# Diagonal row maxima of causal attention: the mask added on VectorE instead of TensorE

## The chip, the cores and the metric

The kernel runs on one core of one Trainium2 chip. The metric is the time of one execution on the device, in microseconds (us), and the median of several. The engines are TensorE (PE in the profile; PEld is its weight loads), VectorE (DVE), ScalarE (ACT), GpSimd (POOL) and SyncE (SP), which issues most DMAs. PSUM is the memory that TensorE writes, in banks of 128 partitions by 512 numbers of 32 bits.

## The reference, cut to what matters

One decoder layer on 2048 tokens of width 256: an embedding whose table is made ternary, an attention block with three branches, and a mixture of eight experts of which two are taken. Only the attention's causal branches bear on the change. There are 16 heads, queries and keys of width 96, values of width 32:

```python
def _attn(q, k, v, causal):
    scale = 1.0 / math.sqrt(q.shape[-1])
    s = jnp.einsum('bhqd,bhkd->bhqk', q, k) * scale
    if causal:
        Tq, Tk = (s.shape[-2], s.shape[-1])
        mask = jnp.tril(jnp.ones((Tq, Tk), dtype=bool))
        s = jnp.where(mask, s, jnp.finfo(s.dtype).min)
    return jnp.einsum('bhqk,bhkd->bhqd', jax.nn.softmax(s, axis=-1), v)
...
a1 = _attn(q, k1, v1, causal=True)
a2 = _attn(q, ks, vs, causal=False)
a3 = _attn(q, kw, vw, causal=True)
out = g[:, 0] * a1 + g[:, 1] * a2 + g[:, 2] * a3
```

`a1` is the branch that the kernel calls LATENT, `a3` is WINDOW, and both cover all 2048 keys with the causal mask. `a2` is SELECT, on 64 chosen keys, without a mask.

## The kernel before

The program runs stage after stage: `embed`, `project`, `select`, `attend` (the 16 heads), `mix`, `experts`. The change lies in `attend`, plus one constant that `embed` makes.

**Two passes over the scores.** A softmax needs each query row's maximum before the exponentials. So `attend` computes the scores twice. The first pass takes maxima only: a max task ("max", h, b, q, c) has queries as PSUM's partitions. It multiplies query block q (128 queries) with up to 512 keys of key block c into one bank of `ps_x` (L1518), and VectorE reduces the bank to one number per query, `max_part[:, q, c]` (L1607). After a branch's last task VectorE folds the parts (L1611), TensorE turns the result (a "neg" task), and it goes by DMA into extra rows of the query operand. The second pass, `pe_scores` (L1485 to L1489), computes the scores again with keys as partitions, three products each since every operand is split into an upper and a lower half. ScalarE takes the exponential twice (L1471, L1473), GpSimd or VectorE subtracts the two for the lower half (L1392), and `pe_values` multiplies both with the values four units later (L1575, L1577).

**The mask.** Where a task's keys reach the diagonal (c == q // 4), the last 128 columns of its w columns are a triangle. TensorE adds the constant `mask_qk` (0 or -1e30) to them by one more product, of `mask_qk` with an identity of bf16 (L1521). w is 128, 256, 384 or 512 in turn. Per head and branch 16 of 40 max tasks are diagonal. The second pass has its own mask product (L1559), with `mask_kq`. The first maxima of head 0 in WINDOW are made in `select`, so `attend` has 31 x 16 = 496 diagonal max tasks.

**Order.** Each engine runs a list written out by hand. A head is 84 units: 44 of WINDOW and SELECT, then 40 of LATENT. In each unit TensorE issues the unit's scores, then the side tasks that `schedule` places there, then the values of four units before. Side tasks are this head's LATENT maxima (units 7 to 37, first half of the head), the next head's SELECT and WINDOW maxima (second half), the "neg" turns, and in heads 0 to 11 the projections for a later group of heads ("prep"). All side tasks share a ring of three banks, `ps_x`: a task waits until VectorE has read the task three before it (semaphore `x_read`). VectorE takes its side tasks in the same order, and between them its share of L1392, the outputs' first addition (L1668), and six steps that finish the head before (L1676 to L1691).

Names in the rows below: `head_first` holds `q_hi`, `q_lo`, `kw_hi` and `kw_lo` of even heads.

Of the kernel before, what the change touches and what calls it, by code (L numbers as in the profile page):

```python
# [12 lines left out]
BF16 = mybir.dt.bfloat16  # L13
I32 = mybir.dt.int32
ALU = mybir.AluOpType
ACT = mybir.ActivationFunctionType
AX = mybir.AxisListType

P = 128
# [12 lines left out]
MASKED = -1.0e30  # L32
CH = 512
# [56 lines left out]
def embed(nc, g, a, x, weight):  # L90
# [7 lines left out]
    with ExitStack() as ctx:  # L98
# [56 lines left out]
        def _(pool):  # L155
# [11 lines left out]
            cst.add(nc.gpsimd.memset(g.mask_kq[:], 0.0))  # L167
            cst.add(nc.gpsimd.memset(g.strict[:], 1.0))
# [6 lines left out]
                                            base=0, pattern=[[1, P]], channel_multiplier=-1))  # L175
            cst.add(nc.gpsimd.affine_select(out=g.strict[:], in_=g.strict[:], compare_op=ALU.is_gt, fill=0.0,
# [892 lines left out]
def attend(nc, g, a):  # L1069
# [7 lines left out]
    with ExitStack() as ctx:  # L1077
# [418 lines left out]
        def pe_task(pe, t):  # L1496

            n = XN[t]
            bank = ps_x[n % NX]
            if n >= NX:  # L1500
                pe.wait_ge(s["x_read"], n - NX + 1)
            if t[0] == "max":
# [8 lines left out]
                if b == SELECT:  # L1511
                    for r in range(8):
                        last = nc.tensor.matmul(bank[:, r * KEEP:(r + 1) * KEEP], q_hi[par][0:DQK, (8 * q + r) * P:(8 * q + r + 1) * P],
                                                ks_hi[par][0:DQK, 0:KEEP], start=True, stop=True)
                else:
                    w = min(CH, (q + 1) * P - c * CH)
                    diag = c == q // 4
                    last = nc.tensor.matmul(bank[:, 0:w], q_hi[par][0:DQK, q * P:(q + 1) * P], k_hi[b][par][0:DQK, c * CH:c * CH + w],  # L1518
                                            start=True, stop=not diag)
                    if diag:  # L1520
                        last = nc.tensor.matmul(bank[:, w - P:w], g.ident16[:], g.mask_qk[:], start=False, stop=True)  # L1521
# [74 lines left out]
        def dve_task(dve, t):  # L1596
            n = XN[t]
            bank = ps_x[n % NX]
            if t[0] == "max":
                _, h, b, q, c = t  # L1600
                dve.wait_ge(s["x"], n + 1)
                if b == SELECT:
                    ins = nc.vector.tensor_reduce(nm[:, NT + 8 * q:NT + 8 * q + 8],
                                                  bank[:].rearrange("p (q k) -> p q k", k=KEEP), axis=AX.X, op=ALU.max, negate=True)
                else:
                    w = min(CH, (q + 1) * P - c * CH)
                    ins = nc.vector.tensor_reduce(mpart[:, q, c:c + 1], bank[:, 0:w], axis=AX.X, op=ALU.max)  # L1607
# [693 lines left out]
def layer(nc, a, out):  # L2301
# [12 lines left out]
    with ExitStack() as ctx:  # L2314
# [3 lines left out]
        g.gates, g.onehot, g.inv = tile("gates", [P, 3]), tile("onehot", [QA, NB]), tile("inv", [P, 1])  # L2318
        with ExitStack() as mid:
# [85 lines left out]
```

## Time and profile before

| | |
|---|---|
| median of 3 runs | 2747.41 us (2745.13 to 2747.56) |
| the profiled execution | 2745.16 us |
| its span in the profile | 2743.4 us |
| TensorE busy | 2327.9 us (85%) |
| VectorE busy | 1815.3 us (66%) |
| ScalarE busy | 1743.7 us (64%) |
| GpSimd busy | 1622.2 us (59%) |

How to read it: a matmul's duration covers its way through the array, so two that follow each other overlap; what one costs the stream is seen from the starts. A row's bracket tells how long the engine had been idle and what ended it. "issue" means that nothing in the profile was waited for. `attend` runs from about 400 to 2340 us; ahead of it come the table scan and the projections, behind it `mix` and `experts`.

### The profile page before, as it was taken

How to read it: one execution, taken by the hardware profiler on the slowest of the kernel's cores; microseconds unless marked ns; L12 is line 12 of the kernel's file. 1: busy time of each engine (PE TensorE's matmuls, PEld its weight loads, DVE VectorE, ACT ScalarE, POOL GpSimd, SP SyncE). 2: the span in 40 equal slices, each digit the busy share in tenths (PEclk: the TensorE clock that was granted, in tenths of full speed). 3: DMA queues.
4: the chain of work that ended last, by engine and by line, in shares of the span. 5: the costliest groups of instructions: out<-in, count | busy, mean ns of one | idle time of the engine just before them, and what ended most of it. 6: DMA issues, size and time to landing. Idle time of an engine off the chain costs nothing. (4 is left out here: it accounts for less than half of the span.)

```text
span 2743.4 us, 38402 instructions
## 1 busy us (share of the span) xinstructions
PE 2327.9 (85%) x12402; PEld 1845.8 (67%) x12402; DVE 1815.3 (66%) x2824; ACT 1743.7 (64%) x3574; POOL 1622.2 (59%) x1430
## 2 busy tenths in 40 slices
PE   0178579999999999999999999999999997538885
PEld 0155346777777777777777777777777775538885
DVE  2557457686776868687776868677686773455553
ACT  3433226777777777777777777777778776116663
POOL 4055316667676666767676666766656665006885
PEclk9985569999999999999999999999999998759998
DMA  9757654325151533414251533232132110615776
GB/s 382 311 187 246 189 127 108 91 68 136 24 154 29 136 66 108 112 48 124 52 142 38 138 69 91 61 67 60 34 67 49 32 25 17 194 62 177 197 203 169
DMA packets 199860, 314.87 MB, mean 115 GB/s; under 512 B 95915, under 2 KB 130219, under 8 KB 186731
## 3 DMA queue, kind: packets, MB, share of 16 engines
q1 hardware_dynamic: 189947, 298.23, 37.9%
q0 software_dynamic: 9712, 14.18, 2.8%
q8 instruction: 99, 1.62, 0.3%
q14 instruction: 102, 0.84, 0.1%
HBM read 210.20 MB, written 101.75 MB: 114 GB/s over the span
## 5 line engine op out<-in xcount | busy, mean ns | idle before, releaser
L1392 POOL TENSOR_TENSOR p_lo<-prob,p_hi 128x512 fp32r<-128x512 f32 (+2 forms) x960 | 1092.3, 1145 | 630.0 <-ACT p_hi L1473 544.7
L1471 ACT ACTIVATE prob<-ps_s 128x512 f32<-128x512 f32 (+4 forms) x1344 | 722.8, 538 | 465.8 <-PE ps_s L1489 303.0
L1607 DVE TENSOR_REDUCE max_part<-ps_x 128x1 f32<-128x128 f32 (+1 forms) x1240 | 713.4, 606 | 195.9 <-PE ps_x L1518 128.0
L1473 ACT ACTIVATE p_hi<-ps_s 128x512 fp32r<-128x512 f32 (+3 forms) x1344 | 718.5, 535 | 1.6
L1392 DVE TENSOR_TENSOR p_lo<-prob,p_hi 128x512 fp32r<-128x512 f32 (+1 forms) x320 | 308.0, 962 | 129.8 <-ACT p_hi L1473 124.4
L1575 PE MATMUL ps_o<-p_hi,v_win 128*128 128x512 f32 (+3 forms) x640 | 251.9, 394 | 8.5 <-DVE p_lo L1392 8.5
L1575 PE MATMUL ps_o<-p_hi,v_lat 128*128 128x512 f32 (+3 forms) x640 | 242.6, 379 | 0.0
L1577 PE MATMUL ps_o<-p_lo,v_win 128*128 128x512 f32 (+3 forms) x640 | 234.6, 367 | 0.0
L1577 PE MATMUL ps_o<-p_lo,v_lat 128*128 128x512 f32 (+3 forms) x640 | 234.1, 366 | 0.0
L1668 DVE TENSOR_TENSOR raw_o<-ps_o,low_sum 32x512 f32<-32x512 f32 x192 | 131.4, 684 | 78.9 <-ACT low_sum L1456 74.5
L1518 PE MATMUL ps_x<-k_hi,head_first 96*128 96x512 f32 (+2 forms) x320 | 120.6, 382 | 29.0 <-DVE max_part L1607 28.0
L1518 PE MATMUL ps_x<-k_hi,q_hi 96*128 96x512 f32 (+2 forms) x320 | 120.8, 383 | 26.7 <-DVE max_part L1607 26.0
L1575 PEld LDWEIGHTS ps_o<-p_hi,v_win 128*128 128x128 f32 x640 | 124.1, 194 | 27.3 <-DVE p_lo L1392 13.7
L1577 PEld LDWEIGHTS ps_o<-p_lo,v_lat 128*128 128x128 f32 x640 | 121.8, 190 | 19.6
L1575 PEld LDWEIGHTS ps_o<-p_hi,v_lat 128*128 128x128 f32 x640 | 122.2, 191 | 18.2 <-POOL p_lo L1392 0.3
L1577 PEld LDWEIGHTS ps_o<-p_lo,v_win 128*128 128x128 f32 x640 | 122.5, 191 | 16.8
L1485 PE MATMUL ps_s<-head_first 97*128 97x512 f32 (+1 forms) x320 | 123.5, 386 | 6.1 <-POOL v_lat L1408 6.0
L1488 PE MATMUL ps_s<-head_first 96*128 96x512 f32 (+1 forms) x320 | 128.1, 400 | 0.0
L2127 POOL DMA_INDIRECT xg<-x_scratch,slot_tok x46 | 51.5, 1120 | 128.6 <-POOLq L1723 118.0
L1488 PE MATMUL ps_s<-q_lo,kw_hi 96*128 96x512 f32 (+1 forms) x320 | 126.5, 395 | 0.0
L1488 PE MATMUL ps_s<-q_lo,k_hi 96*128 96x512 f32 (+1 forms) x320 | 126.1, 394 | 0.0
L1488 PE MATMUL ps_s<-head_first,k_hi 96*128 96x512 f32 (+1 forms) x320 | 126.1, 394 | 0.0
(432 smaller groups left out, 5830.9 us busy)
## 6 DMA issues: line engine op xcount, KB each, us to landing
raw<-in_experts_w_dram SPq DMA_DIRECT2D x23, 1536.0 KB
wbuf<-in_tok_weight_dram SPq DMA_DIRECT2D x16, 2000.0 KB, 16.9
head_first<-kw_scratch SPq DMA_DIRECT2D x72, 256.0 KB, 4.7
kw_scratch<-st_hi SPq DMA_DIRECT2D x48, 256.0 KB, 2.8
kw_scratch<-st_lo SPq DMA_DIRECT2D x48, 256.0 KB, 3.3
q_scratch<-st_hi SPq DMA_DIRECT2D x48, 256.0 KB, 4.8
q_scratch<-st_lo SPq DMA_DIRECT2D x48, 256.0 KB, 5.5
head_first<-q_scratch SPq DMA_DIRECT2D x48, 256.0 KB, 7.5
```

The lines of the kernel that those rows point to most:

```text
L1392: ns.tensor_tensor(upper if low else p_lo[:, i % LSLOTS, c:CH], prob[low:P, i % NPROB, c:CH], upper.bitcast(F32), ALU.subtract).then_inc(s ...
L1471: nc.scalar.activation(prob[low:P, i % NPROB, c:CH], ps_s[i % 3][low:P, c:CH], ACT.Exp, scale=SCALE).then_inc(s["p_full"], 1)
L1473: nc.scalar.activation(p_hi[:, i % SLOTS, c:CH], ps_s[i % 3][:, c:CH], ACT.Exp, scale=SCALE).then_inc(s["p_up"], 1)
L1485: nc.tensor.matmul(out, hi, xhi, start=True, stop=False)
L1488: nc.tensor.matmul(out, hi[0:rows] if rows else hi, xlo, start=False, stop=False)
L1518: last = nc.tensor.matmul(bank[:, 0:w], q_hi[par][0:DQK, q * P:(q + 1) * P], k_hi[b][par][0:DQK, c * CH:c * CH + w], start=True, stop=not ...
L1575: last = nc.tensor.matmul(bank[:, c:CH], w, p_hi[:, i % SLOTS, c:CH], start=(k == 0), stop=bool(low))
L1577: last = nc.tensor.matmul(bank[:, c:CH], w, p_lo[:, i % LSLOTS, c:CH], start=False, stop=output_of(i) is not None)
L1607: ins = nc.vector.tensor_reduce(mpart[:, q, c:c + 1], bank[:, 0:w], axis=AX.X, op=ALU.max)
L1668: nc.vector.tensor_tensor(raw_o[j * DV:(j + 1) * DV, h % 2, br, :], ps_o[BANK[out]][DV:2 * DV, :], low_sum[64 * (j % 2):64 * (j % 2) + DV, ...
L2127: nc.gpsimd.indirect_dma_start(out=xg[i % 2][:, q, :], out_offset=None, in_=g.x2_dram, in_offset=bass.IndirectOffsetOnAxis(ap=g.slot_tok[: ...
```

## The change

`before` is a new constant tile of 128 x 512 in bf16: zeros, and the triangle of -1e30 in its last 128 columns. GpSimd makes it at the start with one memset and one affine select. In a diagonal max task TensorE now issues the product of scores only (`stop=True`), and VectorE runs `tensor_tensor_reduce`: it adds the last w columns of `before` to the bank, writes the sums back into the bank and keeps their maximum. The tasks off the diagonal and the second pass's mask products stay as they are.

```diff
--- before.py
+++ after.py
@@ -165,6 +165,7 @@
 
             cst.add(nc.gpsimd.memset(g.mask_qk[:], 0.0))
             cst.add(nc.gpsimd.memset(g.mask_kq[:], 0.0))
+            cst.add(nc.gpsimd.memset(g.before[:], 0.0))
             cst.add(nc.gpsimd.memset(g.strict[:], 1.0))
             cst.add(nc.gpsimd.memset(g.ones16[:], 1.0))
             cst.add(nc.gpsimd.iota(g.slots[:], pattern=[[1, KEEP]], base=0, channel_multiplier=0, allow_small_or_imprecise_dtypes=True))
@@ -173,6 +174,8 @@
                                             base=0, pattern=[[-1, P]], channel_multiplier=1))
             cst.add(nc.gpsimd.affine_select(out=g.mask_kq[:], in_=g.mask_kq[:], compare_op=ALU.is_ge, fill=MASKED,
                                             base=0, pattern=[[1, P]], channel_multiplier=-1))
+            cst.add(nc.gpsimd.affine_select(out=g.before[:, CH - P:CH], in_=g.before[:, CH - P:CH], compare_op=ALU.is_ge, fill=MASKED,
+                                            base=0, pattern=[[-1, P]], channel_multiplier=1))
             cst.add(nc.gpsimd.affine_select(out=g.strict[:], in_=g.strict[:], compare_op=ALU.is_gt, fill=0.0,
                                             base=0, pattern=[[1, P]], channel_multiplier=-1))
             pool.wait_ge(s["idx"], 16)
@@ -1514,11 +1517,8 @@
                                                 ks_hi[par][0:DQK, 0:KEEP], start=True, stop=True)
                 else:
                     w = min(CH, (q + 1) * P - c * CH)
-                    diag = c == q // 4
                     last = nc.tensor.matmul(bank[:, 0:w], q_hi[par][0:DQK, q * P:(q + 1) * P], k_hi[b][par][0:DQK, c * CH:c * CH + w],
-                                            start=True, stop=not diag)
-                    if diag:
-                        last = nc.tensor.matmul(bank[:, w - P:w], g.ident16[:], g.mask_qk[:], start=False, stop=True)
+                                            start=True, stop=True)
             elif t[0] == "prep":
                 _, gr, what, j, part = t
                 m = NJ * (gr - 1) + j
@@ -1604,7 +1604,10 @@
                                                   bank[:].rearrange("p (q k) -> p q k", k=KEEP), axis=AX.X, op=ALU.max, negate=True)
                 else:
                     w = min(CH, (q + 1) * P - c * CH)
-                    ins = nc.vector.tensor_reduce(mpart[:, q, c:c + 1], bank[:, 0:w], axis=AX.X, op=ALU.max)
+                    if c == q // 4:
+                        ins = nc.vector.tensor_tensor_reduce(bank[:, 0:w], bank[:, 0:w], g.before[:, CH - w:CH], 1.0, -3.0e38, ALU.add, ALU.max, mpart[:, q, c:c + 1])
+                    else:
+                        ins = nc.vector.tensor_reduce(mpart[:, q, c:c + 1], bank[:, 0:w], axis=AX.X, op=ALU.max)
                 ins.then_inc(s["x_read"], 1)
                 if n == LAST_MAX[h, b] and b != SELECT:
                     dve.wait_ge(s["x_read"], n + 1)
@@ -2316,6 +2319,7 @@
         g.ident, g.ones = tile("ident", [P, P]), tile("ones", [P, P])
         g.ident16, g.mask_qk, g.mask_kq = tile("ident16", [P, P], BF16), tile("mask_qk", [P, P], BF16), tile("mask_kq", [P, P], BF16)
         g.gates, g.onehot, g.inv = tile("gates", [P, 3]), tile("onehot", [QA, NB]), tile("inv", [P, 1])
+        g.before = tile("before", [P, CH], BF16)
         with ExitStack() as mid:
             with ExitStack() as front:
                 tile = lambda n, s, d=F32: front.enter_context(nc.sbuf_tensor(n, s, d))
```

On TensorE, in the first half of a head, this is a diagonal task (L1518, L1521) between a unit's last score product and the values of an earlier unit (line numbers move with the diff: L1518 is L1520 after). Before:

```order
L1489 MATMUL ps_s<-head_first 128x512
L1518 MATMUL ps_x<-k_hi,head_first 128x512
L1521 MATMUL ps_x<-mask_qk,ident 128x128
L1575 MATMUL ps_o<-p_hi,v_win 128x512
L1577 MATMUL ps_o<-p_lo,v_win 128x512
```

And after the change:

```order
L1492 MATMUL ps_s<-head_first 128x512
L1520 MATMUL ps_x<-k_hi,head_first 128x512
L1575 MATMUL ps_o<-p_hi,v_win 128x512
L1577 MATMUL ps_o<-p_lo,v_win 128x512
```

The row of the mask product is gone and its neighbours keep their order; 496 such rows leave TensorE's list.

On VectorE, in the stretch where a head's LATENT maxima and the finishing steps of the head before interleave (`row_sums`, `raw_o` and `o_weight` belong to the latter). Before:

```order
L1607 TENSOR_REDUCE max_part<-ps_x 128x1 x3
L1392 TENSOR_TENSOR p_lo<-prob,p_hi 128x512
L1607 TENSOR_REDUCE max_part<-ps_x 128x1 x3
L1685 TENSOR_TENSOR raw_o<-raw_o,o_weight 128x512
L1607 TENSOR_REDUCE max_part<-ps_x 128x1 x2
L1392 TENSOR_TENSOR p_lo<-prob,p_hi 128x512
```

And after (L1608 is the new instruction, L1610 the old):

```order
L1610 TENSOR_REDUCE max_part<-ps_x 128x1
L1608 ISA ps_x,max_part<-ps_x,before 128x512
L1608 ISA max_part 128x1
L1610 TENSOR_REDUCE max_part<-ps_x 128x1
L1395 TENSOR_TENSOR p_lo<-prob,p_hi 128x512
L1610 TENSOR_REDUCE max_part<-ps_x 128x1 x2
L1608 ISA ps_x,max_part<-ps_x,before 128x128
L1608 ISA max_part 128x1
L1688 TENSOR_TENSOR raw_o<-raw_o,o_weight 128x512
L1610 TENSOR_REDUCE max_part<-ps_x 128x1 x2
L1395 TENSOR_TENSOR p_lo<-prob,p_hi 128x512
```

Each diagonal reduction becomes two instructions in the same place: the pass over the bank, and a short one of 128x1 that writes the maximum out.

## Rows read from the trace of the kernel before

**Rows 1.** Busy time of each engine (x instructions), granted clock, in attend and in one head.
```profile
408.00:2319.00 1911.00, 1842.13 (x9374) 1429.09 (x9372) 1390.25 (x2128) 1435.48 (x2962) 1267.12 (x1094) 1.00 0.31 77
1255.30:1377.70 122.40, 118.02 (x600) 91.32 (x599) 90.70 (x139) 91.25 (x189) 82.77 (x72) 1.00 0.38 98
```

**Rows 2.** Who TensorE waited for in attend: us in total, times, longest us.
```profile
PE ps_x L1518 <- DVE max_part L1607: 54.0, 70, 2.2
PEld ps_x L1518 <- DVE max_part L1607: 89.2, 96, 2.7
```

**Rows 3.** Groups by line and shape: count | busy us, mean ns | idle before, releaser.
```profile
L1521 PE MATMUL ps_x<-mask_qk,ident 128*128 128x128 bf16 x496 | 114.9, 232 | 0.0
L1607 DVE TENSOR_REDUCE max_part<-ps_x 128x1 f32<-128x512 f32 x868 | 579.1, 686 | 145.1 <-PE ps_x L1518 128.0 <-PE ps_x L1521 9.3
L1607 DVE TENSOR_REDUCE max_part<-ps_x 128x1 f32<-128x128 f32 x124 | 35.3, 285 | 19.1 <-PE ps_x L1521 17.4
```

**Rows 4.** Timeline of TensorE in head 7: start us, us, what.
```profile
1278.63 0.40 PE L1518 MATMUL ps_x<-k_hi,q_hi 96*128 96x512 f32 x1
...
1279.23 0.39 PE L1577 MATMUL ps_o<-p_lo,v_win 128*128 128x512 f32 x1
...
1281.10 0.22 PE L1575 MATMUL ps_o<-p_hi,v_win 128*128 128x128 f32 x1
...
1281.56 0.39 PE L1485 MATMUL ps_s<-q_hi,kw_hi 97*128 97x512 f32 x1
...
1282.25 0.39 PE L1518 MATMUL ps_x<-k_hi,q_hi 96*128 96x512 f32 x1
...
1282.72 0.40 PE L1577 MATMUL ps_o<-p_lo,v_win 128*128 128x512 f32 x1
...
1299.37 0.23 PE L1518 MATMUL ps_x<-k_hi,q_hi 96*128 96x128 f32 x1
...
1299.80 0.40 PE L1488 MATMUL ps_s<-q_lo,kw_hi 96*128 96x512 f32 x1
```

**Rows 5.** Busy time in stretches of head 7.
```profile
1264.54:1271.26 6.72, 5.96 (x33) 4.09 (x31) 6.42 (x10) 4.90 (x11) 5.29 (x4) 1.00 0.54 155
...
1288.80:1294.10 5.30, 4.66 (x24) 3.38 (x22) 5.20 (x7) 2.34 (x6) 5.15 (x5) 1.00 0.62 203
1295.93:1308.16 12.23, 10.13 (x47) 7.12 (x45) 12.07 (x16) 9.32 (x19) 6.25 (x6) 1.00 1.06 257
```

**Rows 6.** What TensorE's weight loads waited for, second half of head 7.
```profile
PEld ps_s L1559 <- issue: 2.4, 12, 0.3
PEld ps_x L1521 <- issue: 2.0, 10, 0.3
```

**Rows 7.** The same in head 12.
```profile
PEld ps_x L1518 <- DVE max_part L1607: 3.6, 4, 1.8
PEld ps_o L1575 <- DVE p_lo L1392: 0.8, 1, 0.8
```

**Rows 8.** Timeline of VectorE, start us, us: in embed, and in head 7.
```profile
102.44 0.08 DVE L259 DVE_READ_ACCUMULATOR scratch<-scratch 128x1 f32 x1
102.44 0.42 DVE L259 SCALAR_TENSOR_TENSOR scratch<-scratch 128x256 f32<-128x256 f32 x1
102.79 0.08 DVE L259 DVE_READ_ACCUMULATOR scratch<-scratch 128x1 f32 x1
...
1274.95 0.43 DVE L1607 TENSOR_REDUCE max_part<-ps_x 128x1 f32<-128x256 f32 x1
1275.30 0.68 DVE L1392 TENSOR_TENSOR p_lo<-prob,p_hi 128x512 fp32r<-128x512 f32 x1
```

**Rows 9.** One line's instructions on VectorE: ns least/median/most.
```profile
L1668 DVE TENSOR_TENSOR raw_o<-ps_o,low_sum x192: 681/685/689, 405.8 to 2315.3; 32x512 f32<-32x512 f32 x192
...
L1392 DVE TENSOR_TENSOR p_lo<-prob,p_hi x320: 415/860/4381, 391.9 to 2312.9; 128x512 fp32r<-128x512 f32 x128, 128x256 fp32r<-128x256 f32 x32
```

**Rows 10.** Timeline of GpSimd at the start.
```profile
9.71 1.05 POOL L180 DMA_INDIRECT scratch<-in_tok_weight_dram,tok_idx  x1 [4.17 <-DMA tok_idx<-in_x_dram]
```

## The prediction

> **What bounds the kernel now.** I read the busy times by stage first. In attend TensorE is busy 1842 of 1911 us at the full granted clock, while VectorE, ScalarE and GpSimd stand at 1390, 1435 and 1267 us [rows 1]. So the stage goes at the pace of TensorE's instruction stream, and the end of the kernel moves with the end of attend, since mix and experts come behind it and use nothing that is ready earlier. Second, the waits. TensorE and its weight loads wait 54.0 + 89.2 = 143 us in total, and nearly all of it is one wait: the next product into `ps_x` waits for VectorE to read the bank of three tasks before (L1607) [rows 2]. A wait recorded at a weight load counts from the end of the load before, so not all of it is lost; from start to start of the matmuls, a head like head 7 loses some 5.6 us so. They sit in a head's first half. In the second half of head 7 the weight loads wait for no engine at all, only for "issue" ahead of the two kinds of mask products [rows 6]. So there are two regimes: second halves are TensorE's alone, first halves have stretches in which VectorE holds it.
>
> **What the removed product costs TensorE.** 496 products leave, 124 of each width w (L1607 has 124 of 128 columns, and the same of 256 and 384) [rows 3]. Their mean duration of 232 ns is no price, since matmuls overlap. The price is in the starts. With the mask, from L1518 of 512 columns to the second product after the mask it is 1279.23 - 1278.63 = 0.60 us; the same pair without a mask takes 1282.72 - 1282.25 = 0.47 us [rows 4]. The mask costs 0.13 us, which is more than its 128 columns: the next weight load can begin only when the small product starts. For w = 256 and 384, long enough to cover a load as well, I take 0.12 us. For w = 128 the neighbour is itself too short to cover a weight load, so part of the time stays: with the mask 1299.80 - 1299.37 = 0.43 us for a product of 128, the mask and one of 512. Without a mask, two products of 128 and one of 512 took 1281.56 - 1281.10 = 0.46 us; less 0.23 us for the 512 the short ones are 0.115 us each, so one of 128 and one of 512 would be 0.35 us. That leaves 0.08 us. The mean is (0.13 + 0.12 + 0.12 + 0.08) / 4 = 0.112 us, over 496 products **56 us**, or 1.8 us in each half of a head (16 masks). This is the most that TensorE can give back.
>
> **What of it is lost where VectorE holds TensorE.** In head 7 I find five stretches in which VectorE runs without a pause from one event until TensorE is let go: the first of 6.72 us with 6.42 us busy, two of 5.30 and 12.23 us with 5.20 and 12.07 us busy [rows 5], and two shorter ones like them (3.0 and 4.9 us). What TensorE saves inside such a stretch it waits out at its end. They hold four masks (0.45), one of 384 (0.12), one of 128 (0.08), one of 384 (0.12), and in and just ahead of the last one a 512, a 128 and a 256 (0.33): 1.1 us of the 1.8. A head with prep work, of which there are 12, then gains 0.7 + 1.8 = 2.5 us. Heads 12 to 14 have no prep work; there only the last two stretches are left, four waits and one, 3.6 + 0.8 us [rows 7], holding 0.45 us of masks: 3.15 us each. Head 15 has LATENT maxima only: 1.35 us. The sum is 12 x 2.5 + 3 x 3.15 + 1.35 = **41 us**.
>
> **What VectorE gets instead.** The new pair is not in the trace: one pass with a second source in SBUF and its output in PSUM, and a 128x1 instruction that writes the maximum. Call the surplus of a pair over the old reduction d. Nearest row for the pair: in embed an instruction of 256 columns with an accumulator reads it out with 0.08 us, yet the next begins with the read, and the pitch is 102.79 - 102.44 = 0.35 us; the reduction of 256 columns has the same pitch, 1275.30 - 1274.95 = 0.35 us [rows 8]. Nearest row for a source in PSUM and one in SBUF: L1668 took 681 to 689 ns for 512 columns in 192 instances, against a mean of 686 for the reduction of 512 [rows 3, 9]. Both say d = 0, and the bank is free no later than before. From below, d under 0 has nothing for it: every column still passes once. From above: the read and its gap not overlapped, 0.08 + 0.03 us, so d = 0.11; and the pass slowed as L1392 is, a median of 860 ns against the 680 of its like, with many near 1290, where both sources lie in SBUF [rows 9]: (1290 - 680) x 320 / 512 = 0.38 us at the mean width of 320. I take d = 0, by the rows nearest to it. About ten masks of a prep head, three or four of heads 12 to 15, lie in or before a held stretch, some 136 in all; elsewhere VectorE has a quarter of its time free [rows 1]. So the time rises by about 136 x d: 15 us at 0.11, 52 us at 0.38.
>
> The Trainium skill (Vector Engine (DVE) Microarchitecture Reference, Measured stream behaviour on trn2) gives 1.0417 ns a column plus about 75 ns an instruction, for programs of several steps too; an estimate from it for 512 columns is 608 ns of pitch, and by it d would be 0 and the sum unchanged. No row here shows such a program, which is why I cite it.
>
> **What is hidden.** The constant costs GpSimd one memset and one affine select, under a microsecond, ahead of a row where it has idled 4.17 us for the token numbers [rows 10]; without that cover it would be 0.7 us in a stage that waits for the table scan. TensorE's granted clock stays at 1.00, its 2.4 GHz, even in the stretch where it is busy only 10.13 of 12.23 us [rows 5], so a lighter load costs no clock. ScalarE and GpSimd get the same work in less time; at 75% and 66% of attend they are not next. Next is VectorE: in first halves its share of held stretches grows.
>
> **The rivals.**
> A, everything comes: the waits of first halves shrink with the masks, because the events that start the stretches (a `low_sum` copy, a prep product) come earlier as well. For it: half of what I call lost depends on where a stretch is taken to begin. Against it: stretches of 98% busy VectorE cannot be shortened by TensorE. 2747 - 56 = 2691 us.
> B, the pair is longer because the read is not overlapped: d = 0.11, 2747 - 41 + 15 = 2722 us. For it: VectorE writes PSUM nowhere in this trace, and TensorE's ring is released by the read's end. Against it: rows 8.
> C, slower than before: the second source of the pass is held up by GpSimd's reads of SBUF, as L1392 is. With d = 0.38 the time is 2747 - 41 + 52 = 2758 us, and more waits of the three-bank ring would come on top. It decides from d = 41 / 136 = 0.30 us. For it: GpSimd works through attend, and two-source passes with both sources in SBUF do double. Against it: L1668 and its like never did, in 192 instances. The Trainium skill (the same page, Points that are easy to get wrong) says that scalar-tensor-tensor instructions with two SBUF sources that are not bf16 run at half rate. The trace disagrees: L259, with two f32 sources in SBUF, does 256 columns in a pitch of 0.35 us, and here one source is bf16 and one in PSUM. If the rule held all the same, half rate at 320 columns would be d = 0.33 us and 2751 us.
> D, nothing: the pair costs about 0.3 us more by its own overhead and takes back all. 2747 us.
>
> **How the numbers follow.** The profiled execution, 2745.16 us, is 2.3 us under the median; differences count, so I subtract from the median: 2747.4 - 41 = 2706 us. Chances: forecast 0.50, A 0.17, B 0.19, C 0.08, D 0.06. A and B are the sides of the range, and part of the way to D is in it, for values of d between B's and C's: 2688 to 2732 us. 0.2% is 5.5 us, about what a measurement of this kernel can tell from no change. Faster is the forecast, A and B and the near part of D: 0.87; same 0.05; slower 0.08.
>
> **What would show it.** Right: 496 passes of L1608 as long as the old reductions (285 ns at 128 columns, 686 at 512), the reads of some 80 ns starting before the pass's recorded end; TensorE's starts 0.47 us apart where 0.60 stood; second halves of heads with no wait of TensorE for VectorE, each shorter by 1.8 us; waits for L1610 and L1608 a little above 143 us. A prep head would be 2.5 us shorter than its 122.4. Wrong: passes whose durations scatter up to twice (C), a gap of 0.03 us or more between pass and read (B), waits for VectorE that appear in second halves, or waits that fall in the first (A).

## The result and the profile after

The changed kernel takes 2728.06 us in the median of 5 runs, the kernel before, timed beside it, 2745.13 us in the median of 5. The ratio is 0.9931, with a 95% interval of 0.9919 to 0.9943. So it is faster by 17 us, or by 19 us against the median that the prediction started from, where 41 us were forecast. One of the five runs took 2798.52 us, at a mean granted clock of 0.81 against 0.93 in the others, and the ratio leaves it out. The profiled execution of the changed kernel took 2727.35 us, its span 2725.4 us.

All of the difference lies in attend. From the first to the last softmax instruction of ScalarE it took 1923.6 us before (389.4 to 2313.0) and takes 1904.2 now (390.7 to 2294.9), 19.4 us less; the spans of the two traces differ by 18.0. The lengths of the heads, from the first softmax instruction of one to that of the next, in us:

```
heads                      before   after
0                           131.6   130.1
1, 3 to 5, 7 to 9, 11       122.4   121.0
2, 6, 10                    122.4   121.7 (one 121.8)
12 to 14                    114.5   112.8
15                          102.1   102.4
```

Head 0 is left out of what follows where traces are compared: over the ten traces of this study it lasts 125.8 to 134.9 us, with a wait of TensorE for the DMA of a table in it that is between 3.0 and 7.8 us, and with 13 to 29 us at the lower clock.

The windows view of the kernel after, for most of attend: length, then busy time of TensorE, its weight loads, VectorE, ScalarE and GpSimd (x instructions), the granted clock, the DMA share and GB/s. It answers to [rows 1].

```profile
408.00:2310.00 1902.00, 1804.20 (x8895) 1436.10 (x8893) 1425.05 (x2631) 1430.27 (x2968) 1259.09 (x1094) 0.99 0.32 78
```

TensorE is still the fullest engine, at 1804 of 1902 us. VectorE is at 75%, from 73%. The shape of the bound is the one of [rows 1]. The granted clock is 0.99 where it was 1.00, a small number that turns out to matter: of the time at the lower clock in this window some 8 us lie in head 0, and 3.4 us in each of the heads 2, 6 and 10. The same view of head 7, cut where its second half begins, first of the kernel after:

```profile
1248.30:1318.70 70.40, 64.23 (x314) 49.90 (x313) 55.93 (x100) 50.14 (x103) 47.45 (x40) 1.00 0.57 154
1318.70:1369.30 50.60, 50.60 (x256) 41.23 (x255) 36.77 (x72) 40.52 (x86) 34.68 (x32) 1.00 0.14 24
```

and of the kernel before, whose halves the prediction had not shown apart:

```profile
1255.30:1325.50 70.20, 65.82 (x333) 50.13 (x331) 54.95 (x83) 50.42 (x104) 48.07 (x40) 1.00 0.57 154
1325.50:1377.70 52.20, 52.20 (x270) 41.19 (x270) 35.76 (x57) 40.83 (x86) 34.70 (x32) 1.00 0.12 23
```

The second half went from 52.2 to 50.6 us, and TensorE is busy in all of it. The first half went from 70.2 to 70.4 us although TensorE has 1.6 us less to do in it (65.82 to 64.23 busy). Here the gain is lost. Summed from start to start of the matmuls, TensorE's stalls in the first half of head 7 grew from 5.65 us in 8 places to 7.62 us in 9; in head 12 from 3.15 to 4.75 us. In second halves there is none in either kernel.

Who TensorE and its weight loads wait for in attend (us in total, times, longest), to be held against [rows 2]:

```profile
PE ps_x L1520 <- DVE max_part L1610: 47.6, 58, 1.6
PE ps_x L1520 <- DVE max_part L1608: 12.9, 15, 1.1
...
PE ps_x L1540 <- DVE neg_max L1614: 7.7, 12, 0.6
...
PEld ps_x L1520 <- DVE max_part L1610: 77.5, 69, 2.0
...
PEld ps_x L1520 <- DVE max_part L1608: 22.9, 30, 1.5
...
PEld ps_x L1540 <- DVE max_part L1608: 12.5, 12, 1.0
```

The wait for the banks, which was 54.0 + 89.2 us for one line, is now 47.6 + 12.9 on the matmuls and 77.5 + 22.9 on the loads, for the old reductions (L1610) and the new pairs (L1608). New by name is the pair of waits at L1540: 12 times, in heads 1, 3 to 5, 7 to 9 and 11 to 15, and at a matmul that never waited before. L1540 is the product that turns the finished maxima round (`neg_max` of L1614 is its source).

The new instructions on VectorE, as groups by line and shape (count, busy us, mean ns, idle before), to be held against [rows 3]:

```profile
L1610 DVE TENSOR_REDUCE max_part<-ps_x 128x1 f32<-128x512 f32 x744 | 502.0, 687 | 105.1 <-PE ps_x L1520 97.2
...
L1608 DVE CUSTOM_DVE_ANT_0 ps_x<-ps_x,before 128x512 f32<-128x512 f32 x124 | 86.9, 701 | 7.7 <-PE ps_x L1520 5.1
...
L1608 DVE DVE_READ_ACCUMULATOR2_ANT max_part<- 128x1 f32 x496 | 67.1, 135 | 1.1
...
L1608 DVE CUSTOM_DVE_ANT_0 ps_x<-ps_x,before 128x128 f32<-128x128 f32 x124 | 36.5, 294 | 15.1 <-PE ps_x L1520 10.2 <-DVE turned L1656 2.2
```

A pass of 512 columns takes 701 ns against the 687 of the reduction, one of 128 columns 294 against the 285 of [rows 3]. The read of the maximum is recorded with 135 ns rather than 80. Whether that costs pitch is seen in the timeline of VectorE in head 7 (start us, us), the answer to [rows 8]:

```profile
1305.59 0.56 DVE L1608 CUSTOM_DVE_ANT_0 ps_x<-ps_x,before 128x384 f32<-128x384 f32 x1
1306.07 0.14 DVE L1608 DVE_READ_ACCUMULATOR2_ANT max_part<- 128x1 f32 x1
1306.07 0.69 DVE L1610 TENSOR_REDUCE max_part<-ps_x 128x1 f32<-128x512 f32 x1
```

The pass of 384 columns starts at 1305.59, the read at 1306.07, and the next reduction at 1306.07 as well. The pitch is 0.48 us, where plain reductions of 384 columns have 0.47 (the median in the kernel before). The read runs beside the next instruction.

Last, TensorE's starts at what was a masked product of 512 columns, the answer to [rows 4]:

```profile
1308.04 0.39 PE L1520 MATMUL ps_x<-k_hi,q_hi 96*128 96x512 f32 x1
1308.27 0.40 PE L1575 MATMUL ps_o<-p_hi,v_win 128*128 128x512 f32 x1
1308.51 0.40 PE L1577 MATMUL ps_o<-p_lo,v_win 128*128 128x512 f32 x1
```

1308.51 - 1308.04 = 0.47 us, where 0.60 stood with the mask.

So the two kernels differ as forecast in second halves and in the instructions themselves. The first halves have two things in them that the kernel before has not, and each head from 1 to 15 has one or the other.

### The profile page after: what moved, and what is told of

It is laid out like the page before. It is cut to its first block and busy times, and to the rows that moved or that the text cites. A ratio compares the mean times of both kernels' runs of the same rounds, so it can differ in the third digit from the quotient of the medians.

```text
span 2725.4 us, 37909 instructions
## 1 busy us (share of the span) xinstructions
PE 2288.5 (84%) x11906; PEld 1850.5 (68%) x11906; DVE 1848.3 (68%) x3320; ACT 1734.8 (64%) x3574; POOL 1612.8 (59%) x1432
## 5 line engine op out<-in xcount | busy, mean ns | idle before, releaser
L1395 POOL TENSOR_TENSOR p_lo<-prob,p_hi 128x512 fp32r<-128x512 f32 (+2 forms) x960 | 1082.6, 1136 | 619.8 <-ACT p_hi L1476 536.6
L1610 DVE TENSOR_REDUCE max_part<-ps_x 128x1 f32<-128x512 f32 x744 | 502.0, 687 | 105.1 <-PE ps_x L1520 97.2
L1395 DVE TENSOR_TENSOR p_lo<-prob,p_hi 128x512 fp32r<-128x512 f32 (+1 forms) x320 | 310.2, 970 | 127.9 <-ACT p_hi L1476 125.8
L1608 DVE CUSTOM_DVE_ANT_0 ps_x<-ps_x,before 128x128 f32<-128x128 f32 x496 | 244.1, 497 | 49.2 <-PE ps_x L1520 39.4
L1575 PE MATMUL ps_o<-p_hi,v_win 128*128 128x512 f32 (+3 forms) x640 | 238.2, 372 | 8.9 <-DVE p_lo L1395 8.9
L1575 PE MATMUL ps_o<-p_hi,v_lat 128*128 128x512 f32 (+3 forms) x640 | 235.8, 368 | 0.0
L1671 DVE TENSOR_TENSOR raw_o<-ps_o,low_sum 32x512 f32<-32x512 f32 x192 | 131.3, 684 | 78.2 <-ACT low_sum L1459 66.4
L1520 PE MATMUL ps_x<-k_hi,q_hi 96*128 96x512 f32 (+2 forms) x320 | 121.6, 386 | 34.7 <-DVE max_part L1610 24.3
L1520 PE MATMUL ps_x<-k_hi,head_first 96*128 96x512 f32 (+2 forms) x320 | 122.6, 389 | 32.3 <-DVE max_part L1610 23.3
L1577 PEld LDWEIGHTS ps_o<-p_lo,v_win 128*128 128x128 f32 x640 | 123.1, 192 | 19.4
L1575 PEld LDWEIGHTS ps_o<-p_hi,v_lat 128*128 128x128 f32 x640 | 120.8, 189 | 22.1 <-POOL p_lo L1395 0.3
```

Of the source, the lines that this page charges most:

```text
L1395: ns.tensor_tensor(upper if low else p_lo[:, i % LSLOTS, c:CH], prob[low:P, i % NPROB, c:CH], upper.bitcast(F32), ALU.subtract).then_inc(s ...
L1575: last = nc.tensor.matmul(bank[:, c:CH], w, p_hi[:, i % SLOTS, c:CH], start=(k == 0), stop=bool(low))
L1577: last = nc.tensor.matmul(bank[:, c:CH], w, p_lo[:, i % LSLOTS, c:CH], start=False, stop=output_of(i) is not None)
L1608: ins = nc.vector.tensor_tensor_reduce(bank[:, 0:w], bank[:, 0:w], g.before[:, CH - w:CH], 1.0, -3.0e38, ALU.add, ALU.max, mpart[:, q, c:c ...
L1671: nc.vector.tensor_tensor(raw_o[j * DV:(j + 1) * DV, h % 2, br, :], ps_o[BANK[out]][DV:2 * DV, :], low_sum[64 * (j % 2):64 * (j % 2) + DV, ...
```

## In 12 heads: one addition of VectorE that became slow

The last of the six finishing steps of the head before, an addition of 512 columns with both sources in SBUF (L1691 before, L1694 after), stands just ahead of the last maxima of the branch and of the turn at L1540. VectorE, GpSimd and TensorE at this place in head 7, first in the kernel before:

```profile
1315.79 0.69 DVE L1691 TENSOR_TENSOR raw_o<-raw_o 128x512 f32<-128x512 f32 x1
1315.81 1.81 POOL L1392 TENSOR_TENSOR p_lo<-prob,p_hi 128x512 fp32r<-128x512 f32 x1 [0.22 <-ACT p_hi L1473]
...
1316.52 1.29 DVE L1607 TENSOR_REDUCE max_part<-ps_x 128x1 f32<-128x512 f32 x2
1317.84 0.22 DVE L1611 TENSOR_REDUCE neg_max<-max_part 128x16 f32<-128x64 f32 x1
...
1318.86 0.28 PE L1540 MATMUL ps_x<-ident,neg_max 128*16 128x128 f32 x1
```

VectorE's addition starts at 1315.79, 20 ns ahead of a GpSimd instruction, and takes 0.69 us; the GpSimd instruction takes 1.81. The maxima are negated from 1317.84 to 1318.06, 0.8 us ahead of TensorE's product at 1318.86, which waits for nothing. The kernel after:

```profile
1308.61 1.29 POOL L1395 TENSOR_TENSOR p_lo<-prob,p_hi 128x512 fp32r<-128x512 f32 x1
1308.70 1.75 DVE L1694 TENSOR_TENSOR raw_o<-raw_o 128x512 f32<-128x512 f32 x1
1310.48 0.69 DVE L1610 TENSOR_REDUCE max_part<-ps_x 128x1 f32<-128x512 f32 x1
1311.09 0.69 DVE L1608 CUSTOM_DVE_ANT_0 ps_x<-ps_x,before 128x512 f32<-128x512 f32 x1
1311.70 0.14 DVE L1608 DVE_READ_ACCUMULATOR2_ANT max_part<- 128x1 f32 x1
1311.87 0.22 DVE L1614 TENSOR_REDUCE neg_max<-max_part 128x16 f32<-128x64 f32 x1
...
1311.21 0.39 PE L1492 MATMUL ps_s<-q_hi,head_first 96*128 96x512 f32 x1
1312.24 0.27 PE L1540 MATMUL ps_x<-ident,neg_max 128*16 128x128 f32 x1 [0.64 <-DVE neg_max L1614]
```

Now the GpSimd instruction is first, at 1308.61, and takes 1.29 us. The addition starts 90 ns later, takes 1.75 us and ends at 1310.45, which is 0.55 us after GpSimd's end at 1309.90. The maxima behind it are late by that 1.06 us, and `neg_max` is there at 1312.09. TensorE, its last start at 1311.21 and by now free of the masks, stands idle: 1312.24 - 1311.21 = 1.03 us lie between two starts that are 0.23 apart elsewhere, a loss of 0.8 us. Nothing in this addition was changed. Only the phase of two engines was, by some 0.1 us.

How often it happens is told by one line's durations (least/median/most), before and after:

```profile
L1691 DVE TENSOR_TENSOR raw_o<-raw_o x32: 685/693/694, 577.8 to 2330.7; 128x512 f32<-128x512 f32 x32
```

```profile
L1694 DVE TENSOR_TENSOR raw_o<-raw_o x32: 685/693/1753, 577.4 to 2312.4; 128x512 f32<-128x512 f32 x32
```

Before, none of the 32 was slow. After, 12 are, with 1.74 or 1.75 us, in heads 1, 3, 4, 5, 7, 8, 9, 11 and 12 to 15, and in these 12 heads and no other TensorE loses 0.8 us at L1540: 9.6 us.

## In heads 2, 6 and 10: TensorE at its lower clock

These three heads have neither the slow addition nor the wait, and yet they last 0.7 us longer than their neighbours. The windows view of the kernel after has the reason in the granted clock, column behind GpSimd's. First head 2, from 12.5 us ahead of the end of its longest stall to 8 us behind it:

```profile
682.00:694.50 12.50, 10.10 (x45) 7.27 (x43) 12.05 (x18) 9.59 (x20) 6.56 (x6) 1.00 0.26 62
694.50:696.00 1.50, 1.49 (x6) 1.25 (x7) 1.50 (x5) 0.00 (x0) 0.36 (x1) 1.00 0.00 0
696.00:700.00 4.00, 4.00 (x13) 3.14 (x12) 3.58 (x6) 1.96 (x4) 1.40 (x2) 0.57 0.00 0
700.00:704.00 4.00, 4.00 (x18) 3.21 (x17) 3.32 (x6) 3.23 (x7) 2.44 (x3) 1.00 0.00 0
```

and the same place in head 7:

```profile
1288.50:1301.00 12.50, 10.19 (x45) 7.30 (x43) 11.59 (x18) 9.60 (x20) 6.57 (x6) 1.00 1.03 240
1301.00:1302.50 1.50, 1.46 (x6) 1.24 (x7) 1.50 (x5) 0.00 (x0) 0.34 (x1) 1.00 1.00 229
1302.50:1306.50 4.00, 4.00 (x20) 3.21 (x20) 3.91 (x8) 2.78 (x6) 2.41 (x2) 1.00 0.88 203
```

In head 2 TensorE's clock falls to 0.57 of full in the mean of 4 us, which is to say to 1.2 GHz for most of them (3.4 us, in heads 6 and 10 as well): 13 matmuls where head 7 has 20. The first half of head 2 lasts 71.2 us, against 69.6 in the kernel below that has neither trouble, so the fall costs 1.6 us. Ahead of it TensorE was busy 10.10 of 12.50 us in head 2 and 10.19 in head 7, where the clock held; in the kernel before it was 10.46 at the same place of head 7. The change takes busy time out of a stretch whose length VectorE sets. The Trainium skill (TensorE: Matmul & The Clock Gate, Part 1: The HAM clock gate) says that a gate sets the clock by how busy the engine has lately been. The rows agree so far as they go: the fall comes 2 us behind the end of the longest stall of the head, in the kernel with less work there. That of two nearly equal stretches only one was followed by a fall they show and do not explain.

In no trace of this study does a head have both the slow addition and the fall. In head 2 the fall begins at 696.4 us and the turn of the maxima comes at 706.5, so the fall is first. That it moves the engines against each other and so spares these heads the slow addition is likely, but no run tests it.

## The experiments

Each kernel was timed beside the kernel before on the same chip, which took 2745.96 us in the first four and 2746.25 us in the last four. `FINISH` is the table that says after which of a head's units of work VectorE does which finishing step of the head before.

### TensorE's part alone

The mask products are left out, but the diagonal maxima are taken by the old reduction, so they see the masked keys too; that part of the computation is not done.

```
-                    if c == q // 4:
+                    if False:
                         ins = nc.vector.tensor_tensor_reduce(...)
```

> TensorE's half of the change alone: the 496 mask products are left out and all maxima are taken with the old reduction, so the diagonal maxima also see the masked keys (that part of the computation is left out). Theory 1 (the new pair costs VectorE almost nothing; what TensorE saves in first halves of heads is waited out behind VectorE): the time of the changed kernel within 0.25%, 2722 to 2734 us, with first halves of about 70 us and second halves of 50.6 us. Theory 2 (the pair's surplus, from the 496 reads of 135 ns and the later release of the bank, took back the missing 20 us): about 2706 to 2712 us.

Measured: 2721.61 us, ratio 0.9894 (0.9870 to 0.9917). It falls between the theories' numbers, nearer to the first: even with the pair gone the gain is 24 us and not 41. The new wait is there as well, 6 times:

```profile
PE ps_x L1520 <- DVE max_part L1610: 60.1, 72, 2.5
...
PE ps_x L1540 <- DVE neg_max L1614: 3.3, 6, 0.6
```

The slow addition is in heads 2, 4, 6, 8, 14 and 15, and the wait in the same six. In heads 1, 3, 5, 7, 9 and 11 to 13 the clock falls. Head 10 has neither, and lasts 120.1 us. So taking TensorE's work away is enough to make both losses, without the pair. What the pair adds shows in heads of the same kind: 121.0 us against 120.8 here with the slow addition, 121.7 against 121.6 with the fall.

### VectorE's part alone

The mask products stay, and VectorE adds the mask a second time in the pair.

```
                     w = min(CH, (q + 1) * P - c * CH)
-                    ins = nc.vector.tensor_reduce(mpart[:, q, c:c + 1], bank[:, 0:w], axis=AX.X, op=ALU.max)
+                    if c == q // 4:
+                        ins = nc.vector.tensor_tensor_reduce(bank[:, 0:w], bank[:, 0:w], g.before[:, CH - w:CH], 1.0, -3.0e38, ALU.add, ALU.max, mpart[:, q, c:c + 1])
+                    else:
+                        ins = nc.vector.tensor_reduce(mpart[:, q, c:c + 1], bank[:, 0:w], axis=AX.X, op=ALU.max)
```

> VectorE's half of the change alone: TensorE keeps its mask products, VectorE adds the mask once more and takes the maximum with the new pair. Theory 1: the kernel before within 0.25%, 2740 to 2752 us, since the pair starts the next instruction no later than the reduction did. Theory 2: 2757 to 2765 us, the 15 to 20 us that the pair would cost.

Measured: 2751.24 us, ratio 1.0019 (1.0003 to 1.0034): the pair costs 5 us, with an interval of 1 to 9 us. Its instructions are those of the changed kernel, in the groups by line and shape:

```profile
L1611 DVE CUSTOM_DVE_ANT_0 ps_x<-ps_x,before 128x512 f32<-128x512 f32 x124 | 86.9, 701 | 10.5 <-PE ps_x L1524 9.1
...
L1611 DVE DVE_READ_ACCUMULATOR2_ANT max_part<- 128x1 f32 x496 | 66.9, 135 | 1.1
```

In its trace nine of the prep heads last 122.5 us against 122.4, and two 123.1. The addition is slow (1.83 us) in heads 4, 11, 12 and 15, and these four have a wait at the turn of the maxima and are longer by 3.2 us together; the other heads from 1 to 15 are longer by 1.1. The clock falls in none of them. So a head without a collision pays 0.1 us for the pair, and the pair alone can also shift the addition behind GpSimd's instruction, though in four heads and not in twelve. By that, d is 0.1 us over the ten pairs in a prep head's held stretches, 0.01 us each.

### The window branch alone, and the latent branch alone

The change is made for the maxima of one branch only.

```
-                    diag = c == q // 4
+                    diag = c == q // 4 and b == LATENT
...
+                    if c == q // 4 and b == WINDOW:
```

> The change made for the WINDOW maxima alone, which lie in second halves of heads (and the last unit or two of first halves). Theory 1: second halves fall from 52.2 to 50.6 us, first halves keep their 70.1: 15 x 1.6 = 24 us less than before, 2717 to 2724 us, which is faster than the whole change. Theory 2: half of the whole change's gain, about 2735 us.

Measured: 2724.31 us, ratio 0.9913 (0.9889 to 0.9937), with 240 of the 496 masks moved: a gain of 21.6 us, which is not less than that of the whole change. Head 7 in the windows view, its two halves:

```profile
1244.73:1314.77 70.04, 65.73 (x330) 50.21 (x329) 54.81 (x84) 50.29 (x103) 48.06 (x40) 1.00 0.56 154
1314.77:1365.38 50.61, 50.61 (x256) 41.19 (x255) 36.74 (x72) 40.50 (x86) 34.69 (x32) 1.00 0.14 24
```

The second half has its 50.6 us and the first 70.0, 0.2 less for the two window masks in its last units. Its stalls are 5.6 us, as before the change, every prep head lasts 120.6 or 120.7 us, no addition is slow, and from head 1 on no clock falls. The first theory had put 24 us to it. The other half of the change, with the names exchanged in the diff:

> The change made for the LATENT maxima alone, which lie in first halves of heads. Theory 1: first halves stay at 70 to 71 us, second halves at 52.2: 2740 to 2752 us, no gain, with the waits of TensorE for VectorE up by about 2 us a head, 0.8 of them a new wait ahead of the turn of the maxima. Theory 2: about 2735 us.

Measured: 2747.93 us, ratio 1.0001 (0.9988 to 1.0014). 256 masks are gone from TensorE and nothing is gained. All of them lie in first halves. Head 7's first half lasts 70.5 us with 7.61 us of stalls, and among its waits of TensorE there is the new one, 10 times:

```profile
PE ps_x L1543 <- DVE neg_max L1617: 6.4, 10, 0.6
```

Head 10 again has neither trouble and lasts 122.0 us: 0.4 us is what the latent masks give there. With the wait at the turn it is 122.7 us, and with the fall of the clock, in heads 1, 5 and 6, 123.5 (head 15 has a fall too). What they save in a head is less than what either costs.

### The finishing steps later

If the first half is where VectorE holds TensorE, then moving work of VectorE out of it should bring the forecast gain back. Five of the six finishing steps go into the second half, and the store of their result is issued behind them. The table is changed in the kernel before and in the changed one alike.

```
-        FINISH = {20: 0, 27: 1, 29: 2, 31: 3, 33: 4, 35: 5}
+        FINISH = {20: 0, 46: 1, 50: 2, 54: 3, 58: 4, 62: 5}
...
-                if h:
-                    store_output(h - 1)
-                else:
+                if not h:
                     load_ks(1)
                 store_rows(h, 0)
                 store_sums(h, 2)
...
                 store_sums(h, 0)
+                if h:
+                    store_output(h - 1)
```

In the kernel before:

> The kernel before, with the five finishing steps on raw_o moved from units 27 to 35 (first half of a head, where VectorE holds TensorE) to units 46 to 62 of the same head, and the DMA that stores their result moved behind them in SyncE's list. Theory 1: of the 5.6 us of waits in a first half the last four (3.4 us) mostly go; at 15 heads 30 to 50 us, 2695 to 2717 us. Theory 2 says nothing of it.

Measured: 2724.36 us, ratio 0.992 (0.990 to 0.994). The gain is 22 us, less than was expected. A prep head lasts 120.8 us, its first half 68.5 us with 4.07 us of stalls, its second still 52.2. The starts of TensorE in head 7 tell where the missing part is. Of the four last stalls of a first half only the last, of 1.5 us, is gone; the three ahead of it are there as before (0.8, 0.5 and 0.6 us now, 0.9, 0.6 and 0.6 then). 15 x 1.5 = 22 us is what was measured. So the moved steps were not what makes those three.

In the changed kernel:

> The changed kernel with the same move. Theory 1: with VectorE's load spread, the removed products come through: the gain over the unchanged kernel with the same move is 35 to 52 us instead of 18, so 2650 to 2675 us. Theory 2 (the pair's cost): the gain between the two stays at 15 to 22 us, about 2685 us.

Measured: 2684.38 us, ratio 0.9766 (0.9745 to 0.9788). It is the fastest kernel of the study, 44 us below the changed one and 62 below the kernel before. Head 7:

```profile
1227.81:1295.70 67.89, 63.80 (x314) 50.05 (x313) 50.42 (x95) 50.40 (x104) 47.20 (x40) 1.00 0.58 156
1295.70:1346.27 50.57, 50.57 (x256) 41.15 (x255) 39.83 (x77) 40.50 (x86) 35.17 (x32) 1.00 0.15 29
```

Every head from 1 to 11 lasts 118.4 or 118.5 us, heads 12 to 14 last 110.2, and in none is there a slow turn or a fall of the clock. Against the kernel of the run above, which differs by the change alone, the gain is 40 us in the medians. In the traces heads 1 to 15 give 34 us of it (11 x 2.3 + 3 x 2.7 + 1.0); the rest is head 0, of which I make nothing. The forecast had 38.3 us for these heads. The first theory had the gain between the two kernels right (35 to 52 us) but not the time (2650 to 2675 us), since the kernel it starts from was slower than expected; the second had the time and not the gain.

The reason that the first theory gives is not borne out either. The first half still gives back only 0.6 us (68.5 to 67.9) of the 2.0 us of masks in it, as in the run below, where the steps stay. What came back is that neither event happens. The last two additions are slow here in every head from 1 to 14 (0.87 and 1.29 us), and it costs nothing, since they lie in second halves, where TensorE waits for nothing.

### Only the last finishing step later

The run above moves much. This one moves the one addition, from unit 35 to unit 38, behind the last maxima and their negation, and leaves the other steps where they are.

```
-        FINISH = {20: 0, 27: 1, 29: 2, 31: 3, 33: 4, 35: 5}
+        FINISH = {20: 0, 27: 1, 29: 2, 31: 3, 33: 4, 38: 5}
```

In the kernel before:

> The kernel before with only the last finishing step moved from unit 35 to 38, behind the last LATENT maximum. Theory 1: no wait ahead of the turn of the maxima existed here, so little changes: 2738 to 2748 us.

Measured: 2747.98 us, ratio 1.0002 (0.9992 to 1.0011): no change, the addition was not in the way there.

In the changed kernel:

> The changed kernel with the last finishing step moved from unit 35 to 38. Theory 1: the new wait of 0.8 us a head ahead of the turn of the maxima goes, 16 x 0.8 = 12 us less than the changed kernel, 2712 to 2720 us. Rival: the wait comes from the read that the last fold now waits for (0.09 us later), not from the slow addition ahead of it; then the time stays at 2722 to 2730 us.

Measured: 2714.55 us, ratio 0.9885 (0.9867 to 0.9903): 13.5 us less than the changed kernel. The durations of the addition and TensorE's waits, as in the views of the kernel after:

```profile
L1694 DVE TENSOR_TENSOR raw_o<-raw_o x32: 680/689/694, 572.4 to 2297.1; 128x512 f32<-128x512 f32 x32
```

```profile
PE ps_x L1520 <- DVE max_part L1610: 47.5, 58, 1.6
PE ps_x L1520 <- DVE max_part L1608: 13.0, 15, 1.1
```

No addition is slow, and the wait at L1540 is gone from the list, while the waits for the banks are to 0.1 us those of the changed kernel (47.6 and 12.9). So the slow addition was the cause of the new wait. Had the wait come from the pair's later end, it would have stayed, since the pair is as it was. That the addition was in the way by its ordinary 0.69 us, slow or not, is excluded by head 10 of the products-out and of the latent-only kernel: there it stands at its old place, is not slow, the clock does not fall, and TensorE does not wait. Head 7:

```profile
1238.35:1307.93 69.58, 64.04 (x314) 49.95 (x313) 55.69 (x100) 50.27 (x103) 47.51 (x40) 1.00 0.56 155
1307.93:1358.51 50.58, 50.58 (x256) 41.15 (x255) 36.74 (x72) 40.51 (x86) 34.69 (x32) 1.00 0.13 23
```

Its first half lasts 69.6 us, 0.6 less than before the change, with 6.85 us of stalls. The prediction had it at 0.7 less, with 5.65 + 1.1 = 6.75. Ten of the eleven heads 1 to 11 last 120.2 us. The fall of the clock did not go away, it changed heads: heads 1, 13 and 15 have it, and head 13 lasts 113.5 us between two of 111.9. Three heads before and three now, so of the 13.5 us the 9.6 of the turn are accounted for, and the rest is head 0 of the trace (126.9 us against 130.1) and not explained.

## Why the prediction was wrong, step by step

**What bounds the kernel: right.** TensorE's stream sets the pace of second halves, VectorE's stretches that of first halves, and the end moved with the end of attend.

**What a mask costs TensorE: right.** The second half of head 7 fell by 1.6 us. It holds 14 masks (the first two of the window, of 128 and 256 columns, lie in the last units of the first half), and 0.08 + 0.12 less than 1.8 us is 1.6. The starts are 0.47 us apart, as was written. "Each shorter by 1.8 us" was loose by those two masks, which count in the first half instead.

**What the pair costs: right.** d was taken as 0. The passes are 9 to 14 ns longer, the pitch is that of the reductions, and heads without a collision pay 0.1 us (122.5 against 122.4, and 120.2 against the 120.1 of the head without it). The heads that can be compared with the kernel without the pair pay 0.1 to 0.2 us. Rival B's mechanism, a read that is not overlapped, did not happen, though its 2722 us is near the measured time. Rival C's did not either: L1608 took 282 to 733 ns in 496 instances, and none was slowed. Rival A's neither, since the stalls of first halves grew and did not shrink.

**What is lost where VectorE holds TensorE: this step failed.** The term was 1.1 us a head; the kernel lost 1.2 us there and 0.8 more in 12 heads. The sum asked which masks lie inside the existing stretches, and that count was good: without the slow addition and the fall of the clock the stalls of head 7 grew by 1.2 us, with 1.1 forecast, and a prep head came to 2.2 us less, with 2.5 forecast. But it took the set of stretches as given. Taking TensorE's products away moves the engines' instructions against each other, and one addition of VectorE, which had started 20 ns ahead of GpSimd's, now starts behind it and lasts 1.06 us longer, at a place where TensorE can't cover that. So the waits for L1610 and L1608 came to 160.9 us where "a little above 143" was written, and 20.2 us at L1540 came on top. The prediction named "waits that fall in the first" halves as a sign against it, but looked for none that could arise there. [Rows 9] had what was needed. L1392 with a median of 0.86 us and many near 1.29, where 0.68 is its like, said that passes with two SBUF sources hang on what GpSimd does. The prediction used it to bound the pair, to which it does not apply, and did not ask which of the old passes sit just ahead of something TensorE waits for.

**The clock: wrong.** "A lighter load costs no clock" was read from [rows 5], where it is 1.00 with 10.13 of 12.23 us busy. That was true of the kernel before. Behind a stretch with 10.10 of 12.50 us busy it fell, and so in three heads. The step from "holds now" to "will hold with less" had nothing under it.

**GpSimd's constant: right.** It costs 0.7 us ahead of the wait for the token numbers, which shrinks from 4.17 to 3.47 us, and the instruction behind it starts at 9.72 us where it was 9.71. Attend starts 1.3 us later than before; over the ten traces its start lies between 387.0 and 392.2.

**The sum, again,** from the traces, head by head. What the forecast had over the measured 19.4 us, in us:

```
slow addition and its wait            12 heads x 0.8               9.6
fall of the clock                      3 heads x 1.5               4.6
prep heads, 2.2 rather than 2.5       11 heads x 0.3               3.3
heads 12 to 14, 2.6 rather than 3.15   3 heads x 0.55              1.7
head 15, 0.5 rather than 1.35                                      0.9
head 0, 1.5 rather than 2.5                                        1.0
together                                                          21.1
```

The sizes for heads 1 to 14 are those of the heads without either event in the last kernel above. For head 15, which has no such head to compare, 0.5 is its measured -0.3 with the 0.8 of the addition given back. The forecast's 41 less 19.4 is 21.6, the rest being rounding. Two thirds of the miss are the two events that it had no line for, one third is that its sizes were a little high. The measured 2728.06 us still lies between 2688 and 2732, and that is luck: the upper part of that range was there for a dearer pair, and the time is not there for that reason.

**What stays open.** Why the clock fell behind a stretch with 10.10 us of work and not behind one with 10.19, and so which heads will have it, no run tells; it changed places with each edit. Over the ten traces it fell from head 1 on in four kernels: the changed one, products-out (8 heads), latent-only (4) and the changed one with the last step later (3). These four lack the latent mask products and keep the last stall, of 1.6 us. The six others have those products or lack that stall, and none has a fall. No run varies the stall alone at fixed work, so this is a pattern and not a cause. What holds TensorE in the three stalls that moving the steps did not remove was not looked for.

## What to carry to other kernels

What an instruction costs in the pace-setting engine says what can be gained; how much of it comes must be read where another engine holds it, and there one looks not only at the waits that are, but at the instructions whose duration depends on a neighbour and that stand within a few tenths of a microsecond of being waited for. A part of a change that gives nothing alone can be told by making each half of it: here half of the products carried the whole gain. When the gain falls short, list the lengths of the repeated pieces of the program: here prep heads took 121.0 and 121.7 us in one kernel and 120.2 in another with the same work, and each length had one cause.

## What the runs showed of the hardware

**VectorE with two SBUF sources against GpSimd.** In the trace of the kernel after, between 408 and 2250 us, 291 VectorE instructions of 512 columns with both sources in SBUF (L1395, L1688, L1694) start while a GpSimd tensor-tensor instruction runs. Their duration goes with what is left of the GpSimd instruction, with a correlation of 0.9999 in that trace. Over the 260 such instructions of the kernel before it is 0.75, but without two in head 0 (4.38 and 2.55 us, not explained) it is 0.9998. The means, in ns, with those two:

```
left of GpSimd's instruction     0-300   300-600   600-900   900-1300
VectorE's duration, after          744       992      1269       1682
VectorE's duration, before         853       981      1294       1657
```

Those that start with GpSimd idle (126 after, 146 before) take 686 ns in the mean. So VectorE waits out GpSimd's instruction and then needs 0.55 us (545 to 572 ns in all 291). Instructions with a source in PSUM (L1671, L1608, L1610) are not held so: at 512 columns they take at most 686, 733 and 693 ns while GpSimd runs, and 689, 700 and 693 while it does not. It holds the other way round too. The GpSimd instruction that began 20 ns after VectorE's took 1.81 us, the one that began 90 ns ahead of it 1.29 us; and in the trace of the kernel after 138 GpSimd instructions of L1395 with 512 columns start within such a VectorE instruction and take 1.52 us in the mean, 446 others 1.29. The Trainium skill (SBUF — State Buffer, SBUF: two separate sides) says that the two engines share a pair of ports as an exclusive lock, that whichever starts first has it for its whole instruction while the other blocks, and that a VectorE instruction with two SBUF inputs takes it against a GpSimd instruction that reads SBUF. This case's rows agree where they bear on it: 0.69 us for the addition that came first and 1.75 us for the one that came second, and the two groups of GpSimd instructions. The prediction had not drawn on it.

**The accumulator's read.** With 135 ns recorded for a read in the mean of 496, the next instruction started with the read and not after it (1306.07 both, above). A duration in the groups view is no price here; the pitch is.
